# Tiles of one or two half units, more parts, and the second expert product in float32, in a mixture-of-experts and attention kernel on one core

## The chip, the cores and the metric

One core of a Trainium2 chip runs the whole program. The metric is the device time of one execution in microseconds (us). The engines are TensorE (PE, with its weight loads as PEld), VectorE (DVE), ScalarE (ACT), GpSimd (POOL) and SyncE (SP). Here SP issues every plain and every transposing DMA, and POOL every indirect (scattering) one.

## What is computed

`x` is (32, 256, 128) float32, 8192 rows of 128. Three blocks follow one another, each on the result of the one before:

```
x = x + 0.5 * ffn(layernorm(x))     # pass 0
x = x + attn(layernorm(x))
x = x + 0.5 * ffn(layernorm(x))     # pass 1, the same weights
```

`attn` has 16 heads of 8 channels; a row attends to itself and the 8 rows before it in its sequence. `ffn` is a mixture of 8 experts. A row takes the two with the largest router logits, weighted by their softmax probabilities; an expert is

```
h = gelu(row @ W1[e] + b1[e])      # 128 -> 512
y = h @ W2[e] + b2[e]              # 512 -> 128
```

## The kernel before, in words

**Groups and parts.** The rows lie in SBUF in four groups of 2048. In each pass they are routed group by group. Each row has two choices, so a group gives 4096 (row, expert) pairs. Two groups form a part (`PARTS = ((0, 1), (2, 3))`, line 58). The pairs of a part are sorted by expert by scattering them into `x_sorted` in HBM, 32 indirect DMAs of 128 rows for a group (`scatter_rows`, line 555). A row goes there as a high and a low float16 half. In pass 1 POOL waits for the landing after each burst of four (`BURST`).

**Tiles.** When both groups of a part are scattered, `plan` (DVE, line 1264) works out which expert each tile of 256 sorted slots has. An expert's last tile may be part empty, so a part is planned for its worst case, 39 tiles. There are 4 parts over both passes, so 156 tiles. For a tile:
- SP (`load_x`, line 436) reads the tile's first row into a register, issues one transposing DMA into `xsT` (line 440, a ring of 4) and one small DMA for the row numbers and gates (line 444, a ring of 8).
- PE, `up` (line 927): per chunk of 128 of the 512 hidden channels three float16 products of 256 columns (high by high, and the two cross terms), 12 in all. W1 and W2 are held as high and low float16 in `w_hl`.
- ACT: gelu (line 738), four instructions of 256 columns, into `h_f` in float32; then a cast to float16 (line 744), two of 512 columns.
- DVE, `split_h` (line 1347): the float32 value less its float16 half, two of 512 columns.
- PE, `down`: the bias (line 938), then (line 948) per chunk and half of the tile three float16 products of 128 columns, 24 in all.
- DVE, `take_y` (line 1355): times the gate, into `y_sb` (a ring of 4).
- POOL, `scatter_y` (line 572): two indirect DMAs into `y_pairs`, 128 rows each.

**After a part.** `load_y` (SP) waits until every tile of the part is scattered, then loads the pairs back. `combine` (DVE, lines 1107 and 1109) adds them to the rows. In pass 0 the group's attention follows: normalising (ACT, line 590), query, key and value (PE, lines 826 and 829), products of queries and keys and of weights and values on DVE (lines 1132 and 1176), their sums on PE against an identity (lines 843 and 856), and the projection (lines 866 and 873). Line 1204 adds the result. Then the group is routed for pass 1.

**The order.** Each engine runs one in-order queue. Its streams of work (`r` routing, `h` the halves of the rows to be scattered, `e` tiles, `a` attention, `p` combining and preparing, `s` and `y` POOL's two scatters, `t` SP's tile loads) are written out by hand: one letter of `PE_ORDER`, `DVE_ORDER`, `ACT_ORDER`, `POOL_ORDER` and `SP_ORDER` (lines 65 to 102) is one step of a stream, and `take_turns` issues them so. A step whose wait is not met holds all that stands behind it on its engine.

## Time and profile before

| | |
|---|---|
| median of 3 runs | 1198.52 us (1195.54 to 1204.46) |
| the profiled execution | 1194.16 us |
| its span in the trace | 1192.4 us |
| mean granted TensorE clock | 0.866 |

The span is from the first to the last instruction that the trace shows; the execution's own time is 1.8 us longer. A window row gives the stretch and its length, then for each engine the busy us and in brackets the number of instructions, and last the granted clock of TensorE as a share of its full 2.4 GHz, the DMA engines' busy share and GB/s. "Issue" is time in which an engine waited for nothing that the profile shows.

### The profile page before, as it was taken

The numbers are of one execution on the slowest core, as the hardware profiler recorded it, in microseconds if no ns is written. First come the engines' busy times: TensorE is split into PE (matmuls) and PEld (weight loads), VectorE is DVE, ScalarE is ACT, GpSimd is POOL, SyncE is SP. The second block draws the span as 40 slices with busy tenths as digits, with TensorE's granted clock in tenths as the row PEclk, the third lists the DMA queues.
The fourth block names the chain that finished last, engine by engine and source line by source line (L and its number), as shares of the span: only waits on it lengthen the run. The fifth ranks groups of instructions, "written<-read, shape, count | busy, mean of one in ns | idle before, by whom it ended". The sixth has DMA issues, their size and how long they took to land.

```text
span 1192.4 us, 25209 instructions
## 1 busy us (share of the span) xinstructions
PE 871.4 (73%) x7573; PEld 708.8 (59%) x7573; DVE 766.5 (64%) x1366; ACT 666.7 (56%) x1408; POOL 665.9 (56%) x595
## 2 busy tenths in 40 slices
PE   1633086529898989998877978979998783298991
PEld 1523065318676767877766656657786662187781
DVE  4565344216457789579996898679875472056664
ACT  4533186419779666267714621367628673197890
POOL 2386677777775313206665305636675765676672
PEclk9755599759999999999987978989998887598996
DMA  8421143224457110002142002113214341146656
GB/s 267 127 82 48 52 99 75 74 60 89 111 113 155 56 28 23 10 14 53 29 134 72 16 1 67 33 43 72 58 43 71 74 99 54 47 84 163 147 126 213
DMA packets 168050, 94.86 MB, mean 80 GB/s; under 512 B 138893, under 2 KB 151738, under 8 KB 167156
## 3 DMA queue, kind: packets, MB, share of 16 engines
q1 hardware_dynamic: 149748, 57.54, 20.8%
q0 software_dynamic: 18176, 35.72, 10.3%
q8 instruction: 70, 1.15, 0.4%
q14 instruction: 56, 0.46, 0.1%
HBM read 25.78 MB, written 50.59 MB: 64 GB/s over the span
## 4 chain that ended last, share of the span: by engine, by line
PE 25%; DVE 16%; issue 8%; POOL 8%; DMA 8%; SPq 4%; ACT 3%; POOLq 0%; ACTq 0%; DVEq 0%
POOL x_sorted L555 7%; PE bank L948 6%; PE bank L927 6%; DMA x_sorted<-hl,slots_all 5%; PE bank L856 5%; PE bank L843 4%; DVE prod L1132 3%; DVE h_hl L1347 2%; DVE prod L1143 2%; SPq L440 2%; PE bank L829 2%; DMA y_in<-y_pairs 2%; DVE prod L1176 2%; ACT h_f L738 1%; POOL y_pairs L572 1%
## 5 line engine op out<-in xcount | busy, mean ns | idle before, releaser
L572 POOL DMA_INDIRECT y_pairs<-y_sb,tile_ids x312 | 363.2, 1164 | 281.8 <-issue 242.8
L555 POOL DMA_INDIRECT x_sorted<-hl,slots_all x256 | 294.6, 1151 | 223.1 <-DVE hl L1027 92.4
L738 ACT ACTIVATE h_f<-bank,b_cols 128x256 f32<-128x256 f32 x624 | 261.2, 469 | 142.4 <-PE bank L927 125.9
L927 PE MATMUL bank<-xsT,w_hl 128*128 128x256 f16 x1872 | 250.8, 285 | 83.5 <-DMA xsT<-x_sorted 70.9
L948 PE MATMUL bank<-w_hl,h_hl 128*128 x3744 | 249.4, 224 | 64.2 <-DVE h_hl L1347 64.1
L1347 DVE TENSOR_TENSOR h_hl<-h_f,h_hl 128x512 f16<-128x512 f32 x312 | 212.2, 687 | 110.1 <-ACT h_hl L744 106.8
L948 PEld LDWEIGHTS bank<-w_hl,h_hl 128*128 128x128 f16 x3744 | 218.5, 100 | 88.0 <-issue 70.3
L927 PEld LDWEIGHTS bank<-xsT,w_hl 128*128 x1872 | 182.2, 102 | 117.1 <-issue 90.3
L744 ACT CAST h_hl<-h_f 128x512 f16<-128x512 f32 x312 | 192.9, 618 | 9.9
L856 PE MATMUL bank<-prod,ident 128*128 128x256 f32 x576 | 143.2, 408 | 16.5 <-DVE prod L1176 15.0
L856 PEld LDWEIGHTS bank<-prod,ident 128*128 128x128 f32 x576 | 116.5, 206 | 37.1 <-DVE prod L1176 18.9
L1355 DVE TENSOR_TENSOR y_sb<-bank,tile_ids 128x256 f32<-128x256 f32 x156 | 65.7, 421 | 80.4 <-issue 45.8
L662 ACT COPY qkv<-bank 128x384 f32<-128x384 f32 (+1 forms) x96 | 41.2, 444 | 77.4 <-PE bank L829 37.0
L1132 DVE TENSOR_TENSOR prod<-qkv 128x2304 f32<-128x2304 f32 x32 | 81.5, 2549 | 0.3
L1176 DVE TENSOR_TENSOR prod<-score,qkv 128x2304 f32<-128x2304 f32 x32 | 81.5, 2548 | 0.1
L843 PE MATMUL bank<-prod,ident 128*128 128x288 f32 x256 | 63.9, 407 | 0.4 <-DVE prod L1132 0.4
L938 PE MATMUL bank<-b_hl,ones_b 64*128 x156 | 44.4, 284 | 20.9 <-DVE y_sb L1355 20.7
L843 PEld LDWEIGHTS bank<-prod,ident 128*128 128x128 f32 x256 | 48.2, 190 | 14.7 <-DVE prod L1132 1.0
L647 ACT CAST hl<-xn_r 128x1024 f16<-128x1024 f32 x20 | 20.8, 1039 | 59.9 <-DMA x_sorted<-hl,slots_all 59.9
L1016 DVE TENSOR_TENSOR hl<-xn_r,hl 128x1024 f16<-128x1024 f32 x20 | 24.4, 1222 | 46.1 <-ACT hl L647 46.1
L938 PEld LDWEIGHTS bank<-b_hl,ones_b 64*128 64x128 f16 x156 | 14.5, 93 | 57.7 <-issue 57.1
L829 PE MATMUL bank<-wqkv,xnT_p 128*128 128x384 f32 x128 | 47.0, 492 | 0.0
(151 smaller groups left out, 825.1 us busy)
## 6 DMA issues: line engine op xcount, KB each, us to landing
y_in<-y_pairs SPq DMA_DIRECT2D x24, 512.0 KB, 4.2
y_pairs<-y_sb,tile_ids POOLq DMA_INDIRECT x312
x_sorted<-no_rows SPq DMA_DIRECT2D x32, 144.0 KB
x_sb<-in_L_attn_x SPq DMA_DIRECT2D x4, 1024.0 KB, 6.3
x_sorted<-hl,slots_all POOLq DMA_INDIRECT x256
qkv<-y_pairs SPq DMA_DIRECT2D x8, 512.0 KB, 6.8
xsT<-x_sorted SPq DMA_TRANSPOSE x156
tile_ids<-x_sorted SPq DMA_DIRECT2D x156, 2.0 KB
```

What stands on the lines that cost most here:

```text
L555: pool.indirect_dma_start(out=x_sorted[p], out_offset=bass.IndirectOffsetOnAxis(ap=slots_all[:, at:at + 1], axis=0), in_=hl[:, c % 2, i // ...
L572: pool.indirect_dma_start(out=y_pairs, out_offset=bass.IndirectOffsetOnAxis(ap=tile_ids[:, t.n % IDS, i, 0:1].bitcast(U32), axis=0), in_=y ...
L738: ins = act.activation(h_f[:, u % H_RING, c % 2, :], bank[h_banks.uses[u][0]][:, (c % 2) * 256:(c % 2 + 1) * 256], ACT.Gelu, bias=b1_cols[ ...
L744: act.copy(h_hl[:, t.par, 0, 2 * b:2 * b + 2, :], h_f[:, u % H_RING]).then_inc(h_hi, 1)
L829: pe.matmul(prep_bank[k % PREPS][:, 0:3 * D], xnT_p[:, k - RADIUS, 1:1 + P], wqkv[:], start=True, stop=True).then_inc(qkv_done, 1)
L843: ins = pe.matmul(score_bank[c % 2][:, 0:JH * W * HEADS].rearrange("p (n h) -> p n h", h=HEADS), ident[:], products[:, :, d, :], start=(d ...
L856: ins = pe.matmul(score_bank[c % 2][:, 0:JH * D].rearrange("p (j d) -> p j d", d=D), ident[:], prod[:, c % 2, :, w, :], start=(w == 0), st ...
L927: ins = pe.matmul(dst, w_flat[:, bass.ds((e * HC + c) * (2 * P) + ws * P, P)], xsT[:, t.ring, s], start=(n == 0), stop=(n == 2))
L948: ins = pe.matmul(into[:, half, :], h_hl[:, t.par, hs, c, mine], w_flat[:, bass.ds(at + ws * D, D)], start=False, stop=(c == HC - 1 and ws ...
L1132: ins = dve.tensor_tensor(prod[:, prod_of[c]], q_ap.to_broadcast([P, JH, W, D]), windows(lo, D), ALU.mult)
L1176: dve.tensor_tensor(prod[:, c % 2].rearrange("p j w (h d) -> p j w h d", d=DK), score[:, lo:lo + JH].rearrange("p j w (h o) -> p j w h o", ...
L1347: dve.tensor_tensor(h_hl[:, t.par, 1, 2 * b:2 * b + 2, :], h_f[:, u % H_RING], h_hl[:, t.par, 0, 2 * b:2 * b + 2, :], ALU.subtract).then_i ...
```

## The change

- **Parts.** Pass 0 has four parts of one group each; pass 1 has three, of two groups, one and one.
- **Tiles.** The unit is 128 slots. A part of one group is planned for 39 units, made up of 15 wide tiles (two units, 256 slots) and then 9 narrow ones (one unit); the part of two groups for 71 units, 31 wide and 9 narrow. Over both passes these are 184 tiles, 121 wide and 63 narrow, and 305 units (before: 156 tiles, 312 units). A narrow tile's four chunks of hidden channels share one PSUM bank: 12 products of 128 columns in `up`, four gelu instructions of 128 columns, one indirect DMA for y. SP issues one transposing and one small DMA for either kind.
- **Down projection.** W2 stays in float32 (`w2_sb`, straight from its DMA). `down` multiplies gelu's float32 output by it, one product for each chunk and unit: 8 for a wide tile, 4 for a narrow one. The casts of line 744 and the subtractions of line 1347 are gone, and with them the semaphores `h_hi` and `h_split`: `down` waits for gelu alone. `h_f` is a ring of 6. The scale of 64 stays with W1 and b2.
- **Plan.** Some 30 small DVE instructions on one partition instead of some 14, seven times instead of four. Of the two sets of weights only W1 is rounded and split.
- **Order.** All five strings are written anew.

```diff
-SPARE = 8
-TAIL = SLOT_TILE
+SPARE = 10
+TAIL = P
-AHEAD = 3
+H_RING = 6
-PARTS = ((0, 1), (2, 3))
+SPLITS = (((0,), (1,), (2,), (3,)), ((0, 1), (2,), (3,)))
...
 POOL_ORDER = (
-    "sssssssssyysyyyyyysyysyysssyyyyyyyyyyyyyyyyyyysyyyyyyyyyyyyyyyyyyyyyyyyyyyyyyyyyyyyyyyyyyyyyyyssssssssssssssss"
-    "yyyyyysyyyysssyyyysysyyysyyyyyysyyyyyyyyysysssssssyyyyyyyyyyyyyyyyyyyyyyyyyyyyyyyyyyyyyyyyyyyy"
+    "sssssyyyyyssyyyyyyyyyyysyyyyyyyysyyyyyyyyyyysyyyyyyyysysyyyyssyyyyyysyyyyysyyyyyyyyyyyyyyyyyyysyyysssssssyyyyy"
+    "yyyyyyyyyyssssssssyyyyysyysyysysssyyyyyyyyyyysysyyyysyyyyyyyyysssyyyyyyyysyyyyyyyyysyyyyyyyssyyyyyyyyyyyyyyyyy"
+    "yyyyyyyyyyyy"
 )
...
+    UNITS = [(2 * GROUP * len(gs) - E) // P + E for gs in PARTS]
+    WIDE = [(n - E) // 2 for n in UNITS]
+    HT = [n - w for n, w in zip(UNITS, WIDE)]
...
-        w_hl = sb("w_hl", [P, BLOCKS, 2, P], F16)
+        w1_hl = sb("w1_hl", [P, BLOCKS, 2, P], F16)
+        w2_sb = sb("w2_sb", [P, BLOCKS, D], F32)
...
-                    for b in range(2):
-                        u = 2 * t.n + b
+                    for b in range(t.halves):
+                        u = t.u + b
                         act.wait_ge(h_done, u + 1)
                         if u >= H_RING:
-                            act.wait_ge(h_split, u - (H_RING - 1))
+                            act.wait_ge(y_done, tile_of_unit[u - H_RING] + 1)
...
-                        act.wait_ge(h_gelu, u + 1)
-                        if t.n >= 2:
-                            act.wait_ge(y_done, t.n - 1)
-                        act.copy(h_hl[:, t.par, 0, 2 * b:2 * b + 2, :],
-                                 h_f[:, u % H_RING]).then_inc(h_hi, 1)
...
                     for c in range(HC):
-                        if c % 2 == 0:
-                            pe.wait_ge(h_split, 2 * t.n + (c // 2 + 1))
-                        at = (e * HC + (c + E * HC)) * (2 * D)
-                        for ws in range(2):
-                            for half in range(2):
-                                mine = slice(half * P, (half + 1) * P)
-                                for hs in range(2 - ws):
-                                    ins = pe.matmul(into[:, half, :], h_hl[:, t.par, hs, c, mine],
-                                                    w_flat[:, bass.ds(at + ws * D, D)], start=False,
-                                                    stop=(c == HC - 1 and ws == half == 1))
+                        if c % t.per == 0:
+                            pe.wait_ge(h_gelu, t.u + (c // t.per + 1))
+                        for half in range(t.halves):
+                            ins = pe.matmul(into[:, half, :], h_part(t, c // t.per)[:, c % t.per, half * P:(half + 1) * P],
+                                            w2_flat[:, bass.ds((e * HC + c) * D, D)], start=False,
+                                            stop=(c == HC - 1 and half == t.halves - 1))
```

The strings fix where a stage can stand among the others. Counted letter by letter, with x0 to x7 for the eight groups' scatters of 32 DMAs (x0 to x3 in pass 0) and "tile" for the y of a tile on the engine named:

| in the order of | before | after |
|---|---|---|
| POOL: y of the first tile after | 72 DMAs of `scatter_rows` | 40 |
| DVE: attention of group 0 begins after | tile 55 of 156 | tile 44 of 184 |
| POOL: issued up to and with the y of tile 40 | | 80 DMAs of `scatter_rows`, 70 units of y |
| DVE: attention of group 3 ends after | tile 93 | tile 108 |
| POOL: issued up to and with the y of tile 106 | | 204 DMAs of `scatter_rows`, 176 units of y |
| POOL: x7 begins after | tile 111 | tile 122 (224 DMAs, 208 units) |
| POOL: y between the first and the last DMA of x7 | 1 tile | 33 tiles (53 units) |
| PE: steps of tiles in attention, group 0's first to group 3's last | 158 | 228 (some 106 units) |

## Rows read from the trace of the kernel before

**Rows 1.** The page, part 1: busy us (share of the span) and instructions.
```profile
PE 871.4 (73%) x7573; PEld 708.8 (59%) x7573; DVE 766.5 (64%) x1366; ACT 666.7 (56%) x1408; POOL 665.9 (56%) x595
```

**Rows 2.** Windows by stage: PE, PEld, DVE, ACT, POOL busy, clock, DMA, GB/s.
```profile
47.00:97.00 50.00, 14.11 (x73) 12.63 (x73) 33.28 (x92) 19.54 (x28) 39.55 (x32) 0.50 0.22 71
148.00:343.00 195.00, 134.47 (x1505) 109.41 (x1505) 79.80 (x140) 122.84 (x255) 152.00 (x142) 0.84 0.37 83
343.00:402.00 59.00, 53.40 (x591) 42.84 (x591) 45.02 (x104) 53.34 (x124) 32.46 (x31) 1.00 0.62 139
402.00:892.00 490.00, 430.07 (x2837) 343.09 (x2836) 412.25 (x583) 245.08 (x528) 217.13 (x158) 0.94 0.16 43
892.00:975.00 83.00, 69.22 (x780) 57.25 (x778) 46.91 (x117) 67.20 (x145) 54.97 (x54) 0.92 0.39 73
975.00:1037.00 62.00, 15.04 (x161) 12.24 (x161) 13.91 (x27) 12.59 (x25) 35.39 (x37) 0.63 0.20 63
1037.00:1163.00 126.00, 120.26 (x1393) 99.80 (x1393) 77.20 (x130) 107.42 (x230) 86.33 (x80) 0.94 0.57 126
1163.00:1192.40 29.40, 3.68 (x52) 2.87 (x50) 12.69 (x20) 2.44 (x6) 6.65 (x7) 0.60 0.61 215
```

**Rows 3.** Groups by form: line, engine, shapes, count, busy us, mean ns, idle before.
```profile
L572 POOL DMA_INDIRECT y_pairs<-y_sb,tile_ids x312 | 363.2, 1164 | 281.8 <-issue 242.8 <-DVE y_sb L1355 19.5 <-DMA x_sorted<-hl,slots_all 19.2
...
L738 ACT ACTIVATE h_f<-bank,b_cols 128x256 f32<-128x256 f32 x624 | 261.2, 469 | 142.4 <-PE bank L927 125.9 <-DVE h_hl L1347 9.0 <-issue 1.5
...
L948 PE MATMUL bank<-w_hl,h_hl 128*128 x3744 | 249.4, 224 | 64.2 <-DVE h_hl L1347 64.1
...
L1347 DVE TENSOR_TENSOR h_hl<-h_f,h_hl 128x512 f16<-128x512 f32 x312 | 212.2, 687 | 110.1 <-ACT h_hl L744 106.8 <-issue 2.7
...
L744 ACT CAST h_hl<-h_f 128x512 f16<-128x512 f32 x312 | 192.9, 618 | 9.9
...
L772 PE MATMUL bank<-ident,prod 128*128 128x128 f32 x32 | 8.3, 428 | 9.4 <-ACT xnT_p L631 5.9 <-ACT prod L590 3.5
```

**Rows 4.** Windows, POOL alone: first line L555, then line L572.
```profile
148.00:343.00 195.00, 66.71 (x64) 0.84 0.37 83
...
148.00:343.00 195.00, 85.29 (x78) 0.84 0.37 83
```

**Rows 5.** The chain of waits, one burst of L555: start us, us, what.
```profile
605.09 0.95 POOL x_sorted L555
606.35 2.66 DMA x_sorted<-hl,slots_all
```

**Rows 6.** Timeline of POOL, near the end: start us, us, what.
```profile
1169.21 0.98 POOL L572 DMA_INDIRECT y_pairs<-y_sb,tile_ids  x1 [0.31 <-issue]
```

**Rows 7.** Timeline of SP's queue, two tiles in succession.
```profile
1107.67 1.22 SPq L440 DMA_TRANSPOSE xsT<-x_sorted  x1
...
1110.24 1.22 SPq L440 DMA_TRANSPOSE xsT<-x_sorted  x1
```

**Rows 8.** The chain of waits, runs of TensorE at the full clock.
```profile
344.59 1.31 PE bank L927 x12
...
486.12 7.77 PE bank L856 x36
...
653.36 0.89 PE bank L873 x8
...
1127.07 1.45 PE bank L948 x24
```

**Rows 9.** Groups of DVE in 402 to 892 us.
```profile
L1347 DVE TENSOR_TENSOR h_hl<-h_f,h_hl 128x512 f16<-128x512 f32 x77 | 51.0, 678 | 5.0 <-ACT h_hl L744 4.9
...
L1355 DVE TENSOR_TENSOR y_sb<-bank,tile_ids 128x256 f32<-128x256 f32 x38 | 15.8, 416 | 2.1 <-PE bank L948 2.0
L1016 DVE TENSOR_TENSOR hl<-xn_r,hl 128x1024 f16<-128x1024 f32 x12 | 14.6, 1219 | 12.5 <-ACT hl L647 12.5
L1195 DVE TENSOR_TENSOR o_sb<-bank,sinv 128x256 f32<-128x256 f32 x32 | 13.2, 418 | 21.9 <-PE bank L856 21.8
```

More of the change, by code:

```diff
@@ L159, in macaron @@
     G = N // (P * J)
+    PARTS = [gs for parts in SPLITS for gs in parts]
+    PASS = [f for f, parts in enumerate(SPLITS) for _ in parts]
     NP = len(PARTS)
@@ L169, in macaron, with y_moves @@
     REGION = [GROUP * len(gs) + TAIL for gs in PARTS]
-    SLOTS = [E * n + SPARE * SLOT_TILE for n in REGION]
-    PART_OF = [p for p, gs in enumerate(PARTS) for g in gs]
+    SLOTS = [E * n + SPARE * P for n in REGION]
+    PART_OF = [[p for p in range(NP) if PASS[p] == f and g in PARTS[p]][0] for f in range(2) for g in range(G)]
     LOW_SEQ = S // J
-    MAX_GROUPS = max(len(gs) for gs in PARTS)
-    ALL_TILES = [Tile(f, p, at, FIRST, IN_MAP, NT) for f in range(2) for p in range(NP) for at in range(HT[p])]
+    ALL_TILES = [Tile(p, at, WIDE, FIRST, IN_MAP) for p in range(NP) for at in range(HT[p])]
+    for t in ALL_TILES[1:]:
+        t.u = ALL_TILES[t.n - 1].u + ALL_TILES[t.n - 1].halves
+    tile_of_unit = [t.n for t in ALL_TILES for _ in range(t.halves)]
+    def y_moves(ring, n):
+        return DMA * sum(t.halves for t in ALL_TILES[:n] if t.ring == ring)
     x_sorted = [nc.dram_tensor(f"x_sorted{p}", [SLOTS[p], ROW // 2], F32, kind="Internal").ap() for p in range(NP)]
@@ L479, in load_last @@
                     for s in range(4):
-                        sp.wait_ge(y_scattered[s], 2 * DMA * len(range(s, 2 * NT, 4)))
+                        sp.wait_ge(y_scattered[s], y_moves(s, NT))
                     sp.wait_ge(attn_added, G * CH)
@@ L489, in results @@
                     yield from load_y(0, g)
-                for p in range(NP - 1):
+                for p in range(len(SPLITS[0]), NP - 1):
                     for g in PARTS[p]:
@@ L570, in scatter_y @@
                     carry_waits(pool)
-                    for i in range(2):
+                    for i in range(t.halves):
                         pool.indirect_dma_start(
@@ L714, in routes @@
                     if q == PARTS[0][-1]:
-                        for part in range(2):
-                            round_weights(part)
-                            yield
+                        round_weights()
+                        yield
             def prepares():
@@ new lines, in plan @@
+                did(dve.tensor_tensor(units[:, 0, :], counts[:], units[:, 1, :], ALU.subtract))
+                for k in range(2):
+                    did(dve.tensor_tensor(m.sums[:, k], earlier[0:1, :].rearrange("o (e f) -> o e f", f=E),
+                                          units[:, k, :].rearrange("o (e f) -> o e f", e=1).to_broadcast([1, e1, E]), ALU.mult))
+                did(dve.tensor_reduce(starts[:].rearrange("o k e -> o (k e)"),
+                                      m.sums.rearrange("o k e f -> o (k e) f"), X, ALU.add))
@@ new lines, in plan @@
+                did(dve.tensor_scalar(counts[:, 0:1], starts[:, 0, E:e1], float(2 * WIDE[p]), None, ALU.max))
+                did(dve.tensor_scalar(starts[:, 1, :], starts[:, 1, :], counts[:, 0:1], None, ALU.add))
+                offs = row_off[:, 1:].rearrange("o (k e) -> o k e", k=2)
+                did(dve.memset(row_off[:, 0:1], 0.0))
+                for k in range(2):
+                    did(dve.scalar_tensor_tensor(out=offs[:, k], in0=starts[:, k], scalar=-float(P), in1=start,
+                                                 op0=ALU.mult, op1=ALU.add))
```

320 lines of the change are left out of this document (153 added, 167 removed).

## The prediction, made before the changed kernel ran

> **What bounds the kernel now.** I read first the page's busy shares. No engine is full: PE 73%, DVE 64%, ACT and POOL 56% [rows 1]. So the answer must lie in the stages, and I cut the span where the source's waits cut it [rows 2]. (1) To 148 us the first part's two groups are routed and scattered; the first 32 DMAs end at 97, but tiles may start only after 64. (2) 148 to 343: the first part's 39 tiles. GpSimd is the bound. A scattering DMA shows about 0.98 us and has 0.31 us of issue before it, 1.29 us from one to the next [rows 6]; for those of line 555 it is 1.26 [rows 5]. This stage holds 64 of the one and 78 of the other [rows 4]: 64 x 1.26 + 78 x 1.29 = 181 of its 195 us. Wall time there is 1.077 times POOL's work. (3) 343 to 402: loading y, combining, norms, the first queries and keys, 59 us. (4) 402 to 892, 490 us: attention of the four groups, DVE 412 us busy and PE 430, POOL 217. DVE and PE hand work to each other, as DVE's 21.9 us of waiting for line 856 shows [rows 9]. (5) 892 to 1037: routing group 3 for pass 1 and its 32 DMAs with a landing wait for each burst (2.66 us, rows 5), 62 us in which PE is busy for only 15. (6) 1037 to 1163: the last 39 tiles, 3.23 us each, PE busy 120 of 126. (7) 29 us of last y, combining and storing. The times weigh by chain: attention waits for a whole part's y, and the last part's tiles for the last group's scatter.
>
> **The down projection.** Removed for each tile: 24 products, 1.45 us, 60 ns each as the chain has them [rows 8]. Over 3744 that is 226 us. Added: 305 units x 4 = 1220 float32 products of 128 columns. Line 873 is the same form (a fresh float32 operand loaded each time, 128 float32 columns moving): 8 in 0.89 us, 111 ns [rows 8]. So 1220 x 0.111 = 135 us, and TensorE gives up 91 us. What would make it cost more: line 772's float32 products took 428 ns each by their mean [rows 3], but they stand in a stretch at half clock, and that is duration, not spacing. I take 111, the same form, and keep 428 as the far end; less than 60 is excluded, as no row of 128 columns is faster. `up` goes on at 1.31 us for 12 products of 256 columns [rows 8]; 305 units for 312 take 2% off it. A wide tile is then 1.31, a bias of 256 float16 columns like one of `up`, 0.11, and 8 x 0.111 = 2.31 us of TensorE together, where it was 1.31 + 0.11 + 1.45 = 2.87, a narrow one half of that.
>
> A rule speaks against this. The row shows that 256 float32 columns take 7.77 / 36 = 216 ns and 128 take 111, against 60 and 109 (1.31 / 12) for float16 [rows 8]: twice float16's time. The Trainium skill, FP8 and Floating Point Precision, TensorE Precision Notes, says that true FP32 takes four passes through the array. By that rule a product of 128 columns would take 4 x 60 = 240 ns and the 1220 of them 293 us, 67 more than what goes; by the row it is 135. The trace of before disagrees with the rule, in three forms of float32 product, so I go by the row and hold the rule as a rival.
>
> **Casts and subtractions.** ACT loses 312 casts, 193 us, and DVE 312 subtractions, 212 us [rows 3]. They were not the last to come where POOL bounds (stage 2), so there they are worth nothing but a shorter way through a tile (one cast 0.62 and one subtraction 0.69 behind each gelu). In attention DVE spent 51.0 us on 77 of them [rows 9]: this is on the path. ACT's gelu is 4 x 0.419 (261.2 / 624) = 1.68 us a wide tile; a narrow one has four of half the width, between 0.84 and 1.68. Either is under what POOL or SP need for it, so I put it at nothing; if that cover went, 63 narrow tiles could cost up to 63 x 0.84 = 53 us of ACT.
>
> **Tiles and SP.** Two successive transposes are 2.57 us apart when SP waits for nothing [rows 7]. That is 2.57 us a tile whatever its size; a smaller transpose may be quicker, so a narrow tile lies between 1.29 (POOL's one DMA) and 2.57. I take 2.57, since reading the register and issuing don't shrink. 184 x 2.57 = 473 us is no bound for the whole, but it is one for the last part: 24 tiles x 2.57 = 62 us against 39 x 1.29 = 50 for POOL. POOL's total hardly moves: 256 x 1.26 + 305 x 1.29 = 716 us (before 725).
>
> **Parts, and the new order.** Here lies the gain. Tiles start after 32 DMAs rather than 64, at about 100 us. By the order, attention of group 0 begins on DVE at tile 44; y_sb is a ring of 4, so POOL has then done tile 40: 80 - 32 = 48 DMAs and 70 units since 97 us, 60 + 90 = 151 us, x 1.077 = 162. With 6 us of handing on, attention begins at 265 us instead of 402. The other conditions are earlier: part 0's y is complete after 32 DMAs and 39 units, 97 + 91 x 1.077 = 195, plus stage 3's 59 = 254.
>
> Attention itself (490 us): DVE's 412 busy us lose 51.0 and gain 26 more y (64 for 38), 11 us at 0.42 each and less for narrow ones, say 9; one more group's halves, 4 x 1.22 [rows 9] and their small copies, 6 us; one more group's combining, 8 at 0.63 (12.69 / 20, rows 2), and its norm, 10 us; one more plan, 10 us by estimate (some 30 instructions, smaller than line 1355's 0.42 [rows 9], say 0.33 each; between 0 and 13). That is 396. Of the 78 us that DVE stood idle I keep 60, as the two handovers inside each tile are gone. PE's tile work grows: 106 units x 1.16 = 123 us for 38 tiles x 2.87 = 109, so its 430 becomes 444. It makes 456 us. POOL has (204 - 80) x 1.26 + (176 - 70) x 1.29 = 293 us of work there, plus some 24 landings; it fits. Bounds: DVE without any idle, 396; the old stage plus the 14 us of PE and 60 us of waits for POOL's queue, 564.
>
> After attention (at 265 + 456 = 721): before, x7 began 83 us after it. By the order POOL has then to go from about tile 106 to 122, 20 DMAs and 32 units, 67 x 1.077 = 72. Then x7 is shared: 32 x 1.26 + 53 units x 1.29 + 8 landings x 2.66 = 130 us (before it stood alone in 57). Then 5 us as before, 24 tiles x 2.57 = 62 and 8 from the first load to the last y, and the end: 21 us after the last y in stage 7 for 8 chunks, 16 for 4. The sum is 721 + 72 + 130 + 5 + 70 + 16 = 1014 us of span, 1016 with the 1.8 us around it, for the profiled 1194.16. The median of the runs shown is 0.4% above that execution, so I say **1020**.
>
> **Rivals.**
> - **Attention shrinks to DVE's work.** For it: PE and ACT have shorter tiles. Against: 50 us of DVE's idle time was PE's own attention sums. At 405 us for the stage it is 51 less: 969.
> - **POOL's queue slows attention.** For it: POOL goes from 217 busy us to about 290 plus landings, and every engine is in order, so a late y or burst holds DVE's attention behind it. Against: DVE's idle rows in that stage name PE. At 560 us for the stage: 1124.
> - **Nothing comes of it.** If the in-order queues let part 1's tiles crowd out attention so that it still starts near 400, only the removed work counts: about 1190. Against: all conditions of its start are met by 265.
> - **Slower: the float32 products.** If a product takes 428 ns [rows 3], a wide tile is 1.42 + 3.42 = 4.84 us of PE, and PE bounds. To tile 44 that is 74 units x 2.42 = 179 at full clock and some 210 with the half-clock stretches (165 now); in attention 106 units cost 257 instead of 123; behind it 125 units cost 303 where 270 were to be had. 1020 + 45 + 134 + 33 and about 30 more of handing on = 1262. Of the 387 us of PE added, 242 are on the path; by that share it decides from about 340 ns, where 281 are added and 176 take the whole gain. The rows' 111 stands against it.
> - **Each float32 product takes four float16 ones' time.** 4 x 60 = 240 ns [rows 8] adds (0.240 - 0.111) x 1220 = 157 us to PE, of which by a somewhat smaller share, since PE then only just bounds, 90 are on the path: 1110. Against it: no float32 row shows more than twice float16's time. This is what the rule of the Trainium skill named above would do here.
>
> **How the numbers follow.** Forecast 0.62, shorter attention 0.17, POOL's queue 0.10, four products' time 0.04, nothing 0.02, slower 0.05. A measurement of this kernel tells about 1% from no change. Faster by over 1% is 0.62 + 0.17 + 0.10 + 0.04 = 0.93, within 1% is 0.02, slower is 0.05. The range leaves out the slow cases and half of each neighbour: 940 to 1100.
>
> **What would show it.** Line 948's successor: 1220 products, 8 in 0.9 us. No CAST on `h_hl`. First y of a tile near 108 us. DVE's first line-1132 instruction near 265 and its last line-1204 near 720, with under 80 us idle between. SP's transposes 2.57 apart in the last part, narrow tiles too. POOL over 65% of the span. The prediction is wrong if attention still starts after 330, if that stage takes over 540 us, if the products are over 0.2 us apart, or if x7 is over long before the second part's y.

## The result, and the profile after

The changed kernel takes 1127.2 us (median of 5 runs, 1124.3 to 1133.1) against 1196.4 (5 runs) for the kernel before, measured beside it: ratio 0.941, interval 0.937 to 0.945. It is faster by 5.9%, where the forecast had 15% (1020 us) and the range ended at 1100. The direction was right, the size was not. The profiled execution's span is 1131.4 us where the sum had 1014.

The page's first part after the change, to be laid beside [rows 1]:

```profile
span 1131.4 us, 23018 instructions
...
PE 940.7 (83%) x6633; PEld 790.2 (70%) x6633; DVE 602.0 (53%) x1241; ACT 498.4 (44%) x1215; POOL 654.5 (58%) x593
```

DVE and ACT lost their subtractions and casts as forecast. But PE, which was to give up 91 us, has gained 69. The stages, cut at the same events as [rows 2] (columns as there):

```profile
101.00:279.00 178.00, 157.69 (x1294) 136.25 (x1295) 61.98 (x200) 97.96 (x248) 122.01 (x122) 0.93 0.39 90
...
279.00:833.00 554.00, 504.54 (x3124) 411.79 (x3124) 403.65 (x623) 239.58 (x563) 318.55 (x239) 0.95 0.22 57
833.00:897.00 64.00, 60.11 (x511) 51.95 (x509) 27.29 (x96) 38.90 (x93) 40.68 (x41) 0.99 0.34 72
897.00:1031.00 134.00, 108.27 (x905) 93.45 (x905) 26.97 (x62) 49.70 (x142) 84.01 (x86) 0.89 0.43 112
1031.00:1115.00 84.00, 75.12 (x624) 64.25 (x624) 14.45 (x33) 34.06 (x96) 43.09 (x44) 0.91 0.48 109
```

| term of the sum | forecast | measured | off by |
|---|---|---|---|
| attention starts at | 265 | 279 | +14 |
| attention's stage | 456 | 554 | +98 |
| from there to x7's first scatter | 72 | 64 | -8 |
| x7 | 130 | 134 | +4 |
| to the last y (5 + 70) | 75 | 84 | +9 |
| end | 16 | 16 | 0 |

So nearly the whole miss lies in one stage. Attention began 123 us earlier than before and then took 64 us longer than its 490. The rest of the net gain comes behind it: 300 us before, 298 now, nothing; in front: the 123. 123 - 64 + 2 = 61 us, which is the difference of the two spans. Two readings of that stage follow. First the product that replaced line 948's, in the groups by form:

```profile
L955 PE MATMUL bank<-w_sb,h_f 128*128 x2440 | 338.1, 291 | 0.0
L938 PE MATMUL bank<-xsT,w_hl 128*128 128x256 f16 x1452 | 193.5, 285 | 26.7 <-DMA xsT<-x_sorted 18.4 <-ACT h_f L753 8.1
...
L949 PE MATMUL bank<-b_hl,ones_b 64*128 x184 | 48.9, 266 | 46.5 <-DVE y_sb L1368 46.4
```

2440 instructions stand there for the 1220 products that the source issues: **a float32 product is two MATMUL records.** Read in the chain of waits, in a run in which TensorE waits for nothing (start us, us, what):

```profile
1058.21 1.31 PE bank L938 x12
1059.52 0.21 PE bank L949
1059.73 1.98 PE bank L955 x16
1061.71 1.31 PE bank L938 x12
```

The 12 float16 products of `up` take the 1.31 us of [rows 8], the bias takes 0.21 where 0.11 was forecast, and a wide tile's eight float32 products take 1.98, as 16 records, 0.25 us a product. Eight of line 873's records took 0.89 us [rows 8], so a pair of records, one product, takes 0.223; 16 records at that pace are 1.78, and the run here takes 0.2 more. A wide tile is thus 3.50 us of TensorE, not 2.31. Nor was it 2.87 before: the timeline of the kernel before, in such a run, has the bias at 0.21 too, and 2.97 from one tile's bias to the next one's (start us, us, what):

```profile
1126.79 0.28 PE L938 MATMUL bank<-b_hl,ones_b 64*128 x1
1127.00 1.51 PE L948 MATMUL bank<-w_hl,h_hl 128*128 x24
1128.35 1.47 PE L927 MATMUL bank<-xsT,w_hl 128*128 128x256 f16 x12
1129.76 0.28 PE L938 MATMUL bank<-b_hl,ones_b 64*128 x1
```

There 24 float16 products of 128 columns stand in 1.35 us, 56 ns from one to the next.

Second, what VectorE waited for. The waits of DVE in attention's stage, first the kernel before (402 to 892 us), then the changed one (279 to 833), each as engine, line, releaser: us in total, times, longest:

```profile
DVE o_sb L1195 <- PE bank L856: 21.8, 10, 3.5
DVE score L1153 <- PE bank L843: 16.7, 8, 3.4
DVE hl L1016 <- ACT hl L647: 12.5, 4, 5.8
DVE x_sb L1204 <- PE bank L873: 12.4, 10, 2.1
DVE h_hl L1347 <- ACT h_hl L744: 4.9, 5, 2.6
DVE y_sb L1355 <- PE bank L948: 2.0, 3, 1.0
```

```profile
DVE y_sb L1368 <- PE bank L955: 37.8, 24, 3.8
DVE o_sb L1203 <- PE bank L866: 33.3, 15, 5.3
DVE hl L1024 <- ACT hl L666: 21.8, 7, 5.7
DVE score L1161 <- PE bank L853: 20.4, 10, 4.7
DVE x_sb L1212 <- PE bank L883: 13.9, 10, 3.1
DVE y_sb L1368 <- DMA y_pairs<-y_sb,tile_ids: 5.5, 2, 3.7
DVE y_sb L1368 <- issue: 4.3, 2, 4.0
```

DVE's work in the stage is 404 us, close to the 396 forecast. It is the idle time that is off: 554 - 404 = 150 us, where 60 were kept. The largest new item is y: 48 us in front of line 1368, where 2 stood before. DVE takes y 65 times in the stage, not 38, each time from the one PSUM bank that `down` has there, and in a fixed place of its order.

### The profile page after: what moved, and what is told of

It reads as the page before. It is cut to its first block, busy times and chain, and to the rows that moved or that the text cites. A ratio compares the mean times of both kernels' runs of the same rounds, so it can differ in the third digit from the quotient of the medians.

```text
span 1131.4 us, 23018 instructions
## 1 busy us (share of the span) xinstructions
PE 940.7 (83%) x6633; PEld 790.2 (70%) x6633; DVE 602.0 (53%) x1241; ACT 498.4 (44%) x1215; POOL 654.5 (58%) x593
## 4 chain that ended last, share of the span: by engine, by line
PE 27%; POOL 11%; issue 9%; DVE 9%; DMA 8%; SPq 2%; ACT 0%; POOLq 0%; DVEq 0%; ACTq 0%
PE bank L955 11%; POOL x_sorted L574 9%; PE bank L938 7%; DMA x_sorted<-hl,slots_all 7%; PE bank L866 5%; POOL y_pairs L591 2%; DVE prod L1140 2%; DVE prod L1184 1%; PE bank L853 1%; DVE prod L1151 1%; PE bank L949 1%; SPq L461 1%; PE bank L839 1%; DVE smax L1172 1%; DMA xsT<-x_sorted 1%
## 5 line engine op out<-in xcount | busy, mean ns | idle before, releaser
L591 POOL DMA_INDIRECT y_pairs<-y_sb,tile_ids x305 | 338.9, 1111 | 272.7 <-issue 168.1
L574 POOL DMA_INDIRECT x_sorted<-hl,slots_all x256 | 307.0, 1199 | 188.9 <-issue 76.3
L753 ACT ACTIVATE h_f<-bank,b_cols 128x256 f32<-128x256 f32 (+1 forms) x736 | 265.0, 439 | 337.6 <-PE bank L938 321.9
L955 PE MATMUL bank<-w_sb,h_f 128*128 x2440 | 338.1, 291 | 0.0
L955 PEld LDWEIGHTS bank<-w_sb,h_f 128*128 128x128 f32 x2440 | 300.9, 199 | 19.8 <-issue 1.1
L938 PE MATMUL bank<-xsT,w_hl 128*128 128x256 f16 (+1 forms) x2208 | 249.0, 264 | 29.7 <-DMA xsT<-x_sorted 21.5
L1368 DVE TENSOR_TENSOR y_sb<-bank,tile_ids 128x256 f32<-128x256 f32 (+1 forms) x184 | 69.1, 376 | 322.8 <-PE bank L955 295.4
L938 PEld LDWEIGHTS bank<-xsT,w_hl 128*128 x2208 | 196.4, 102 | 59.1 <-issue 34.8
L681 ACT COPY qkv<-bank 128x384 f32<-128x384 f32 (+1 forms) x96 | 41.5, 448 | 26.7 <-PE bank L839 16.7
L609 ACT ACTIVATE xn_r<-x_sb,shift_r,rstd_r 128x128 f32<-128x128 f32 x96 | 39.3, 486 | 10.4 <-DVE shift_r L1011 10.4
L693 ACT COPY oT<-bank 128x256 f32<-128x256 f32 x32 | 11.7, 374 | 57.2 <-PE bank L876 56.9
```

Of the source, the lines that this page charges most:

```text
L574: pool.indirect_dma_start(out=x_sorted[p], out_offset=bass.IndirectOffsetOnAxis(ap=slots_all[:, at:at + 1], axis=0), in_=hl[:, c % 2, i // ...
L591: pool.indirect_dma_start(out=y_pairs, out_offset=bass.IndirectOffsetOnAxis(ap=tile_ids[:, t.n % IDS, i, 0:1].bitcast(U32), axis=0), in_=y ...
L753: ins = act.activation(h_part(t, b)[:, k, :], bank[h_banks.uses[u][0]][:, k * t.slots:(k + 1) * t.slots], ACT.Gelu, bias=b1_cols[:, bass.d ...
L938: ins = pe.matmul(dst, w1_flat[:, bass.ds((e * HC + c) * (2 * P) + ws * P, P)], slots_of(t)[:, s], start=(n == 0), stop=(n == 2))
L955: ins = pe.matmul(into[:, half, :], h_part(t, c // t.per)[:, c % t.per, half * P:(half + 1) * P], w2_flat[:, bass.ds((e * HC + c) * D, D)] ...
L1368: dve.tensor_tensor(y_sb[:, t.ring, 0:t.halves], y_bank(t), tile_ids[:, t.n % IDS, 0:t.halves, 1:2] .to_broadcast([P, t.halves, D]), ALU.m ...
```

## The experiments

What the altered kernels leave out is said with each. The **stage** is always from DVE's first product of queries and keys (line 1132 before, 1140 after) to its last residual addition (1204, 1212). Ratios are to the kernel before, measured beside each.

**The two halves of the change alone.** e2_parts_alone is the changed kernel with half tiles, parts and orders, but the down projection as it was: casts and splits of h in float16, W2 as two halves, three products (h in rings of 3 and 4 buffers, and the subtractions of some tiles one step earlier in DVE's stream).

```diff
-                            ins = pe.matmul(into[:, half, :], h_part(t, c // t.per)[...],
-                                            w2_flat[:, bass.ds((e * HC + c) * D, D)], start=False, ...)
+                            for ws, hs in ((0, 0), (0, 1), (1, 0)):
+                                ins = pe.matmul(into[:, half, :], h_half(t, c // t.per, hs)[...],
+                                                w2_flat[:, bass.ds((e * HC + c) * (2 * D) + ws * D, D)], ...)
```

> Parts, half tiles and the new order as in the changed kernel, but the down projection as before: gelu in float32, cast on ACT, subtraction on DVE, three float16 products. The steps of DVE's order take the subtractions of the next tile along. TensorE does 3 x 56 = 168 ns where it now does 223, 67 us less in all; ACT does some 190 us more and DVE some 210. Theory P: TensorE bounds and DVE has 40% idle, so it comes out near the changed kernel or below: 1095 to 1130, attention's stage 530 to 555. Rival O: longer ways through a tile and more in DVE's in-order queue make it slower than the changed kernel, 1150 or more.

e3_float32_alone is the kernel before with only the down projection in float32, h in a ring of 6 (`H_RING = 6`) and no `h_hl`.

```diff
-        h_f = sb("h_f", [P, 3, 2, SLOT_TILE], F32)
-        h_hl = sb("h_hl", [P, 2, 2, HC, SLOT_TILE], F16)
+        h_f = sb("h_f", [P, 6, 2, SLOT_TILE], F32)
```

> The kernel before with nothing but the float32 down projection (no casts, no subtractions, h ring of 6); tiles of 256, parts of two groups and the old order. TensorE gets 1248 products of 223 ns for 3744 of 56, 68 us more; ACT loses 193 us and DVE 212. Theory P: where TensorE bounds, it is slower (the last 39 tiles 3.2 us each at least instead of 3.23 with gaps, attention's stage 17 us more of TensorE), where POOL bounds nothing changes: 1190 to 1215. If DVE and ACT had been the bound in attention: 1140 to 1160.

Measured: e2 1195.4 us, ratio 0.9988 (0.9966 to 1.0009); e3 1198.6 us, 1.0003 (0.9973 to 1.0033). Neither half alone is worth anything here, both together are worth 69 us. (Each half ran in an order that was written for another kernel: e2 in the changed kernel's, e3 in the old one's. What either would give in an order of its own isn't shown.) The stage of e2, then that of e3 (windows, columns as above):

```profile
303.00:884.00 581.00, 496.68 (x3554) 391.90 (x3553) 466.98 (x729) 306.09 (x671) 314.96 (x237) 0.94 0.22 54
```

```profile
400.00:889.00 489.00, 442.12 (x2531) 360.38 (x2530) 368.94 (x507) 198.88 (x450) 216.13 (x157) 0.94 0.17 43
```

In e2 attention starts 99 us earlier and ends 8 us earlier than before: DVE must now do 467 us of work in the stage, since the tiles that used to lie in front of attention lie within it. In e3 DVE has 43 us less to do than before and the stage doesn't get shorter: it waits 32.1 us in front of y where it waited 2.0, and 30.8 in front of o_sb (21.8 before). What the casts' removal gave DVE went into waiting for TensorE. The engines of the chain that ended last, from the page of e3:

```profile
PE 51%; POOL 6%; DMA 6%; DVE 6%; issue 6%; ACT 2%; SPq 1%; POOLq 0%; ACTq 0%; DVEq 0%
```

TensorE was 25% of that chain before. So the two halves need each other: the parts move work into attention's stage, and the float32 product takes 63 us of DVE's work out of it again (467 to 404).

**The price of the product.** e1_price_112 is the changed kernel with gelu writing float16 and W2 in two float16 halves: two products of 56 ns instead of one of 223. The low half of h is left out.

```diff
-        h_f = sb("h_f", [P, H_RING, 2 * SLOT_TILE], F32)
+        h_f = sb("h_f", [P, H_RING, 2 * SLOT_TILE], F16)
...
+                            for ws in range(2):
                                 ins = pe.matmul(into[:, half, :], h_part(t, c // t.per)[...],
-                                                w2_flat[:, bass.ds((e * HC + c) * D, D)], ...)
+                                                w2_flat[:, bass.ds((e * HC + c) * (2 * D) + ws * D, D)], ...)
```

> The changed kernel, but gelu writes h as float16, W2 is held as high and low float16, and each product of the down projection is two float16 instructions (h by high, h by low) instead of one float32 product. The low half of h is left out. Two float16 instructions of 128 columns are 112 ns, just the price that the prediction took for a float32 product. Theory P (the product's price): the trace after shows each float32 product as two instructions 111 ns apart, 223 ns, so TensorE has 135 us too many; it bounds the stages. Then this kernel gives most of that back: attention's stage (554 us) falls to 480 to 500, the last 24 tiles from 84 to about 70, and the whole comes to 1030 to 1060. Rival Q (POOL's queue) and rival O (the new order itself holds attention, whatever the product costs): the stage stays over 530 and the whole at 1095 or more.

Measured: 1111.3 us (1108.2 to 1113.0), ratio 0.928 (0.924 to 0.932). Its products cost what the forecast had taken, 112 ns, and it is 16 us faster than the changed one, where the forecast lay 107 under it. The stage is 548 us. The mistake in the price is real and is not what the forecast failed by.

**More and less of it.** c5_half_again issues every second down product twice (610 more, +136 us of TensorE; y then holds those blocks' share twice). e5_half_again is the same kernel on another chip.

```diff
                         for half in range(t.halves):
-                            ins = pe.matmul(...)
+                            for again in range(1 + (c % 2 == 0)):
+                                ins = pe.matmul(...)
```

> The changed kernel with every second chunk's float32 products issued twice: 610 more of 223 ns, 136 us more of TensorE (the output then counts those chunks twice). The run at 112 ns took 135 us of TensorE away and gained only 16. Theory O (no engine bounds attention; its stage is a row of stretches in which now one engine, now another holds the rest in order): a small response on this side too, 1140 to 1170. Theory P: TensorE is already at its bound with 223 ns, so what is added is nearly all paid: 1210 to 1250.

> As e5_half_again: 136 us more of float32 products. On the other chip it took 0.992 of the kernel before. Theory O: 1150 to 1190. Theory P: 1210 or more.

c12_pe_light goes the other way: e1, and of the up projection's three products only the first (high halves alone; the two others are left out). By the rows that is 269 us of TensorE's work less. e12_pe_light is the same kernel on the other chip. c0_changed_again is the changed kernel once more, as a control.

```diff
-                        for n, (ws, s) in enumerate(((0, 0), (0, 1), (1, 0))):
+                        for n, (ws, s) in enumerate(((0, 0),)):
```

> As e12_pe_light: 269 us less of TensorE. On the other chip it took 0.912 of the kernel before and attention's stage 563 us. Theory P: 1000 or less. Theory O or Q: 1085 to 1105 with attention's stage over 520, since the run at 112 ns a product (1111) had already taken what there was to take.

> The kernel at 112 ns a product, and `up` with one float16 product instead of three (the two cross terms and h's low half are left out): TensorE has 135 + 134 us less than the changed kernel. Theory P: if TensorE bounded any stage, it no longer does, and attention's stage falls to DVE's own bound, 430 to 460, the whole to 980 to 1020. Theory O or Q: the stage stays over 510, the whole over 1070.

> The changed kernel itself, as the measure for the three beside it. The last four ran on a chip on which the kernel before takes 1339 us instead of 1197, because all engines but GpSimd stand still together now and then (one such stop in the trace lasts from 432 to 443 us), and there no run of the changed kernel stands beside them. All theories: 0.94 of the kernel before, 1127 where the latter takes 1197.

Measured: c0 1127.8 us (ratio 0.941, 0.937 to 0.945), c5 1214.0 (1.012, 1.008 to 1.017), c12 1101.4 (0.919, 0.915 to 0.923). 136 us more cost 86; 269 less give 26. The response has a knee, and the changed kernel stands near it. Of the 86 only 22 lie in the stage (574 us in c5, 552 in c0); 27 lie before it and the rest behind it. Of the 26 given back 4 lie in the stage and 19 behind it. The engines of the chain that ended last, from the page of c5 and from that of c12:

```profile
PE 48%; DVE 7%; POOL 6%; DMA 6%; issue 6%; ACT 1%; SPq 0%; POOLq 0%; DVEq 0%; ACTq 0%
```

```profile
DMA 14%; POOL 14%; issue 12%; PE 10%; DVE 9%; SPq 7%; ACT 0%; POOLq 0%; DVEq 0%; ACTq 0%
```

With more on TensorE the chain is TensorE's; with less the largest shares are landings and GpSimd's scatters, and the end hardly moves. The stage of c12:

```profile
270.00:818.00 548.00, 455.29 (x2620) 345.01 (x2617) 402.91 (x623) 239.61 (x565) 316.02 (x240) 0.86 0.23 58
```

It is 4 us shorter than c0's 552. TensorE's busy time fell by 46 us only (501 in c0), although the stage lost some 47 us in `down` (424 products, 111 ns less each) and 47 in `up`: the granted clock fell from 0.96 to 0.86 in the stage, and what was left took longer (`add_window`'s 576 records 144.2 us against 135.9 in c0). That accounts for 8 of the 48 us between 94 and 46.

**GpSimd.** c8_pool_light issues one indirect DMA of y for each tile where the changed kernel issues two for a wide one (121 fewer, 156 us; the second half of each wide tile's y is left out, and y_pairs is cleared by a DMA at the start). e8_pool_light is the same on the other chip, e14_both_light is e8 with e1's edit.

```diff
-                    for i in range(t.halves):
+                    for i in range(1):
                         pool.indirect_dma_start(
                             out=y_pairs, ...
```

> As e8_pool_light: 121 fewer indirect DMAs, 156 us of GpSimd. On the other chip it took 0.896 of the kernel before. Theory Q: 1050 to 1075, attention's stage 500 to 530. Theory O or P: over 1085.

> The changed kernel, but GpSimd scatters only the first unit of each wide tile: 121 indirect DMAs of 1.29 us fewer, 156 us of 716. The second unit's y is left out (y_pairs is filled with zeros once at the start, one DMA of 8 MB). Theory Q (POOL): group 0's attention, in which POOL shows 105 us busy and 23 of issue in 134, falls to 110 to 120 us, the whole stage of 554 to about 500, the stretch of the eighth group's scatter (134 us) to below 90, and the whole comes to 1020 to 1050. Theory O or P: attention's stage stays over 530; only the start of attention and the eighth scatter come earlier, the whole 1070 to 1100.

> Both: products at 112 ns and 121 fewer indirect DMAs (the low half of h and the second unit's y of wide tiles are left out). If the two limits stand side by side and each hides the other, the gain is more than the sum of the single ones (16 us for the price): below 1000, attention's stage below 480. If they are independent, it is their sum: about 16 us below the run with fewer DMAs. Theory O (the order alone): attention's stage still over 510.

e4_no_landing_waits drops pass 1's wait for the landing of each burst of four scatters.

```diff
                         if f and (i + 1) % BURST == 0:
-                            pool.wait_ge(rows_scattered[c % 2], ...)
-                            carry_waits(pool)
                             if i + 1 < 2 * JQ:
                                 yield
```

> The changed kernel without POOL's waits for the landing inside a chunk of pass 1's scatters (the chunks' own waits stay). Rival Q: POOL's queue holds attention; without 24 waits there of about 2.3 us its stage falls by 30 to 60 us and the whole to 1060 to 1095. Theory P: attention's stage stays within 15 us of 554, and only the eighth group's scatter, which stands alone on the path for a while, gets shorter by up to 18 us: 1105 to 1127.

Measured: c8 1111.3 us (0.927, 0.923 to 0.931), e4 1112.6 us (0.930, 0.926 to 0.935). Their stages are 545 and 544 us. (Of the 121 DMAs that c8 leaves out, 40 lie in the stage, 52 us at 1.29.) So the rival in which POOL's queue lengthens the stage to 560 us gave the right number, 1124, by luck: its reason accounts for little of it. e4 computes all that the changed kernel computes and is the fastest such kernel of the study.

On the second chip the kernel before took 1339 us, and the traces from there show stops of all engines but GpSimd (in e12, from 432 to 443 us, GpSimd is busy 6.9 us, TensorE 1.5 and the others 0.2 at most); ratios from there aren't compared with the others. They were 0.992 (e5), 0.897 (e8), 0.912 (e12) and 0.869 (0.861 to 0.878) for e14, whose stage is still 558 us there, against 558 for e8 and 563 for e12: light on both engines, and no shorter.

**VectorE, and what hides behind what.** The stage was still not explained, so three more engines' loads were lifted off it in turn. e17_pe_light_no_landings is c12 with e4's edit.

> The changed kernel with TensorE made light as in c12_pe_light (products in float16 with the low half of h left out, one of three products of the up projection kept, so parts of both projections are left out) and without pass 1's waits for a burst's landing. In c12 the chain through attention's stage was made of GpSimd's scatters of x (86 us) and landings (57 us). Landing theory: they were the bound, so without the waits the stage falls from 548 to about 490 and the ratio from 0.919 to about 0.87. DVE theory (its steps in a written order, each waiting for the engine before it): the stage stays within 12 us of 548 and the ratio is 0.90 to 0.92, as the same edit took only 15 us from the changed kernel.

e19_dve_light takes work from DVE: softmax without its maximum, and probabilities times values for 5 of 9 windows (the other 4 windows' values are left out; `WV` is 5).

```diff
-                    at.did(dve.tensor_reduce(smax[:], mine.rearrange("p j w h -> p j h w"), X, ALU.max))
-                    at.settle()
-                    dve.tensor_tensor(mine, mine, smax[:]..., ALU.subtract).then_inc(score_ready, 1)
+                    dve.tensor_copy(smax[:, 0, :], mine[:, 0, 0, :]).then_inc(score_ready, 1)
...
-                    dve.tensor_tensor(prod[:, c % 2].rearrange(...),
+                    dve.tensor_tensor(prod[:, c % 2, :, 0:WV].rearrange(...),
```

> The changed kernel with less work on VectorE in attention: softmax's maximum is neither taken nor subtracted (28 us off by the rows), and the product of probabilities and values covers 5 of 9 windows (36 us off); the other 4 windows' values are left out. TensorE and GpSimd keep all their work. DVE theory: its written order sets attention's stage, so the 64 us come off it one for one: stage 553 to about 489, ratio 0.941 to about 0.888. TensorE theory (its 504 us of the stage, at 223 ns a float32 product, are the bound): the stage falls by 16 us at most, ratio 0.93 to 0.941. Landing theory: within 1% of 0.941.

e20_pe_dve_light has the edits of c12 and e19, e21_all_light those of c12, e19, c8 and e4.

> TensorE as light as in c12_pe_light and VectorE as light as in e19 (parts of both projections and 4 of 9 windows' values left out). If each of the two hides the other's gain: stage from 548 to 480 or less, ratio from 0.919 to about 0.87 or less, while e19 alone shows little. DVE theory: the same 0.87, and e19 alone shows 0.888. Landing theory: stage at 535 to 548, ratio 0.91 to 0.92.

> All three at once: TensorE and VectorE as in e20, one indirect DMA of y per tile instead of up to two, and no waits for landings (the other half of wide tiles' y, parts of both projections and 4 of 9 windows' values left out). Every theory has a gain here; it shows what is left of attention's stage when DVE has about 340 us of work in it: about 400 if the stage follows DVE's work, 470 or more if a fixed chain of handovers (ScalarE's copies among them) is left. Ratio about 0.80 by the first, 0.86 or more by the second.

Measured: e17 1077.8 us (0.898, 0.894 to 0.902), e19 1101.0 (0.917, 0.911 to 0.923), e20 1070.3 (0.890, 0.885 to 0.895), e21 1015.5 (0.846, 0.841 to 0.850). The stages of e19, e20 and e21:

```profile
277.00:802.00 525.00, 494.57 (x3123) 406.39 (x3123) 344.30 (x614) 239.28 (x563) 289.21 (x239) 0.97 0.24 60
```

```profile
270.00:788.00 518.00, 439.93 (x2611) 335.22 (x2609) 343.12 (x615) 238.86 (x563) 291.25 (x239) 0.89 0.24 61
```

```profile
260.00:752.00 492.00, 433.03 (x2614) 329.89 (x2613) 344.13 (x616) 237.89 (x564) 245.97 (x199) 0.91 0.24 59
```

Side by side, with DVE's idle time (stage less its busy time):

| kernel | lighter on | stage us | PE, DVE, POOL busy | DVE idle |
|---|---|---|---|---|
| c0, the control | - | 552 | 501, 403, 317 | 149 |
| c12 | PE | 548 | 455, 403, 316 | 145 |
| c8 | POOL | 545 | 504, 404, 268 | 141 |
| e4 | landings | 544 | 504, 405, 325 | 139 |
| e17 | PE, landings | 540 | 451, 403, 331 | 137 |
| e19 | DVE | 525 | 495, 344, 289 | 181 |
| e20 | PE, DVE | 518 | 440, 343, 291 | 175 |
| e21 | all four | 492 | 433, 344, 246 | 148 |

Within the stage c12 takes some 94 us off TensorE, c8 some 52 off GpSimd and e19 59 off VectorE. VectorE is the only engine whose load alone moves the stage by more than 2%, and the 59 us move it by 27; the other half turns into waiting (149 to 181), half of that before y (41 to 57 us). In e19 GpSimd was busy less too (289 us for 317, its scatters of x 1.17 us each for 1.35); why isn't known, but at the rate of c8, where 49 busy us less gave 7, that would be some 4 of the 27. In none of the eight does DVE idle less than 137 us. Even with all four lighter the stage is 36 us longer than the 456 forecast for the full load. So the idle time is no remainder that one engine's work alone makes. The reading that is left is the order, in which each of DVE's steps follows one of PE's, ACT's or a landing, and those follow DVE's; it is argued from these runs and not shown, since no run changed the order, and TensorE is still busy for 433 of e21's 492 us.

**Taking y off DVE.** Last, the largest of the waits was attacked itself. In e23_y_on_act ScalarE copies y from its bank with the gate as the scale; the copies are put into `ACT_ORDER` as steps of their own, at the places in time at which DVE took y in c0's trace, and DVE's own step does nothing.

```diff
+            def results():
+                for t in ALL_TILES:
+                    act.wait_ge(y_done, t.n + 1)
+                    if t.n >= 4:
+                        act.wait_ge(y_scattered[t.ring], y_moves(t.ring, t.n))
+                    act.wait_ge(ids_loaded[t.n % IDS], (t.n // IDS + 1) * DMA)
+                    for i in range(t.halves):
+                        ins = act.activation(y_sb[:, t.ring, i, :], y_bank(t)[:, i, :], ACT.Copy,
+                                             scale=tile_ids[:, t.n % IDS, i, 1:2])
+                    ins.then_inc(y_ready, 1)
+                    yield
```

> The changed kernel with y taken out of its bank by ScalarE (a copy scaled by the gate, one per 128 slots, put into ScalarE's written order at the places in time where VectorE took it) and not by VectorE. Handover theory: in attention's stage VectorE loses 24 us of work and the 41 us that it stands waiting for the down projection in front of y, so the stage falls from 552 to about 490 and the ratio from 0.941 to about 0.89. TensorE theory (a chain through TensorE's own queue, with 501 of 552 us busy): the 41 us come up again in front of VectorE's other waits for TensorE, the stage falls by 10 to 27 us as it did for 64 us less of VectorE's work, ratio 0.92 to 0.935. Slower if ScalarE's new wait for y holds up its copies: ratio over 0.945.

> The same, and without pass 1's waits for a burst's landing, which alone gave 1112.6 us (0.930). If the two gains are from different waits they add up: 1 to 5% under 1112.6 (0.88 to 0.92, by which theory holds for e23). If both only feed the same chain: within 1% of the better one.

Beside both the kernel before takes 1339 us again, though not on e8's chip but on that of e1 to e4, where it had taken 1197; so that time doesn't belong to one chip. Measured: e23 1285.4 us, 0.962 (0.958 to 0.966); e24, with e4's edit too, 1330.2 us, 0.991 (0.988 to 0.995). The stage of e23 is 589 us, where e8 and e12 have 558 and 563. The changed kernel itself didn't run under these conditions. From the three kernels that ran under both, with their times over c0's (0.985, 0.977 and 1.076), its ratio would be between 0.910 and 0.934, an estimate; e23 lies above it. So no gain shows. But e23's stage holds stops as well: from 450 to 455 us only GpSimd is busy, and single waits of DVE last 25.4, 19.6, 16.7 and 13.9 us where c0's longest is 5.8. What the edit does to the stage without them isn't shown. ScalarE's groups in e23's stage, 357 to 945 us:

```profile
L755 ACT ACTIVATE h_f<-bank,b_cols 128x256 f32<-128x256 f32 (+1 forms) x256 | 94.2, 442 | 90.9 <-PE bank L952 75.2 <-remote 10.2 <-issue 4.7
...
L767 ACT ACTIVATE y_sb<-bank,tile_ids 128x128 f32<-128x128 f32 x106 | 34.7, 371 | 64.3 <-PE bank L969 35.0 <-remote 18.4 <-issue 10.9
```

ScalarE now waits 35 us for the down projection in front of y, as DVE did in c0 (31): that wait moved with the instruction. And DVE's waits for line 880 (`add_window`) and line 897 (the projection) are 39.6 and 31.8 us, where c0 has 32.3 and 15.0. Why e24 is slower than e23, where e4's edit gained 15 us from the changed kernel, wasn't found; the stops may be part of it (in e24's stage single waits of DVE last 24.3 and 23.0 us).

## Why the prediction missed, step by step

**What held.** Attention's start: 279 against 265, since 32 DMAs open the tiles. x7 (134 against 130), the way to it (64 against 72) and the end. DVE's work in the stage, 404 against 396. That the removed casts were worth nothing where POOL bounds (in e3, without them, attention starts at 400 for 402). Of the last part's rule, SP's 2.57 us a tile, half held: for the wide tiles the chain is TensorE's, 3.50 us each, up to 1077 us; then it is SP's queue, whose last nine transposes start 27 us apart from first to last, 3.4 us each with SP's other DMAs among them. The stretch took 9 us more. One of those steps in the chain (line 458 reads the tile's row, 461 is the transpose, 465 the small DMA; start us, us, what):

```profile
1085.52 1.20 SPq L461
1086.92 0.89 SPq L465
1087.86 0.27 SPq L458
1088.16 0.16 SPq L458
1088.53 1.19 SPq L461
```

**The step that failed** is "Of the 78 us that DVE stood idle I keep 60, as the two handovers inside each tile are gone". It was 150. That is 90 of the 117 us between the two sums. The two handovers (cast, subtraction) did go. But they had been a cover: while DVE subtracted, TensorE ran ahead, and y was ready when DVE came to it, 2.0 us of waiting for 38 tiles [rows 9]. With the subtractions gone the next step in DVE's order is y itself, and the wait for TensorE comes up there. Two pairs show it. e3, beside the kernel before: 43 us less work for DVE, 30 more of waiting before y, 9 more before o_sb, and a stage of the same length; but its products also cost TensorE more. e1, beside e2: the same tiles, parts and orders, no casts or subtractions, and products that are cheaper (112 ns for e2's 168), yet DVE waits 36.3 us before y where e2 waits 9.4. So it is not the product's price; c12, with TensorE lighter still, waits 36.8 (c0 40.9). The rows of y in the stage, of e2, e1 and c12:

```profile
L1386 DVE TENSOR_TENSOR y_sb<-bank,tile_ids 128x256 f32<-128x256 f32 (+1 forms) x64 | 23.7, 371 | 9.4 <-PE bank L972 9.4
```

```profile
L1374 DVE TENSOR_TENSOR y_sb<-bank,tile_ids 128x256 f32<-128x256 f32 (+1 forms) x65 | 23.8, 367 | 36.3 <-PE bank L960 30.8 <-DMA y_pairs<-y_sb,tile_ids 4.2 <-issue 0.9
```

```profile
L1374 DVE TENSOR_TENSOR y_sb<-bank,tile_ids 128x256 f32<-128x256 f32 (+1 forms) x65 | 23.9, 367 | 36.8 <-PE bank L960 26.9 <-DMA y_pairs<-y_sb,tile_ids 5.4 <-issue 4.0
```

TensorE's side turns round with it. Before each bias it waits until DVE has emptied y's bank: 34.6 us of e2's stage, 13.3 of the changed kernel's.

And by starting earlier the stage takes in 65 tiles, not 38, with as many more handovers. DVE's idle time in the stage is 78 us in the kernel before, 114 in e2 (more tiles, subtractions kept), 149 in c0 (subtractions gone too; 144 in e1, with the cheaper products): each of the two adds some 30 to 36. The forecast counted the tiles' work on each engine and not what each of them waits for.

**The mis-sized term** is "8 in 0.89 us, 111 ns". Those eight rows of line 873 were records, and two records make one product: [rows 3] shows 3744 records for 3744 float16 products of line 948, so the count told nothing there, but line 873 issues 64 products in the whole kernel and has 128 records. A product takes 223 ns, and TensorE gained 69 us where it was to give up 91; 62 of them are 1220 x 0.223 = 272 us for 3744 x 0.056 = 210. By e1 this is worth 16 us. The 428 ns of line 772, kept as the far end, were another form: line 772 is a transpose, one record for each. The bias, 0.11 in the sum, takes 0.21 in either kernel. The Trainium skill, FP8 and Floating Point Precision, TensorE Precision Notes, gives true FP32 four passes; 223 ns is 4.0 times the 56 ns from one float16 product of 128 columns to the next in the trace of before, so rule and trace agree, and the prediction was wrong to set the rule aside.

**The rivals.** "Each float32 product takes four float16 ones' time" had the price, and its 1110 us came near, but by the wrong share: it put 90 of 157 us on the path, where taking 135 away gives 16. "POOL's queue slows attention" had 560 us for the stage and 1124 in all; some 52 us less on POOL in the stage give 7 us of it, the landings 8. The slower rival put the end of the whole gain at about 340 ns a product; c5, whose products come to 335 ns for each that is needed, is 1.2% slower than the kernel before. It was the knee that was missing from each of them: one price for both directions.

**What stays open.** No single bound of the stage was found. The eight kernels show that work taken off TensorE, GpSimd or the landings alone gives 4 to 8 us of the stage, that DVE's work counts by half, and that 137 us or more of idle time stay in all. Whether another written order would close them wasn't tried. Nor was a second PSUM bank for y: in the stage `down` has one, so that TensorE waits for DVE to empty it (38.7 us in c12) and DVE for TensorE to fill it (26.9).

## What to carry to other kernels

When an instruction that stood between two handovers is removed, ask what the engine's next instruction waits for; the freed time often comes up as a wait there, so keep the idle time of the old stage at least, and more if the stage takes in more handovers. Count a float32 product's records against the products that the source issues before pricing it. Near a balance of two engines, price a change with one slope for more work and another for less: here 0.63 us of time for each us added to TensorE, and 0.10 to 0.12 for each taken away. Count a rival engine's load in the stage that is asked about, not over the whole span: of c8's 156 us only a third lay there.

## What the runs showed that wasn't expected

- A float32 product is two records (a float32 transpose, line 876, is one), 111 to 112 ns apart at 128 columns and 216 at 256 (line 866), so 223 and 432 ns a product.
- Taking work off TensorE lowered its clock: mean granted clock 0.94 for the changed kernel's span, 0.84 in e20 and 0.83 in e17, and in attention's stage 0.96 in c0 against 0.86 in c12. Of some 94 us taken from the stage, 46 came off its busy time.
- A run of products costs more than its spacing says: the bias of 256 columns takes 0.21 us of the chain in both kernels, where a product of its width in `up` takes 0.11, and a wide tile's 16 float32 records take 1.98 where 16 at the pace of line 873 are 1.78 (24 of them, in c5, take 2.88).
